# Reordering one turn of a four-layer conditional network: score products and exponentials, the gate's row and logits, and the turned attention output

## The reference, cut to what matters

```
x = x + (einsum('bnh,boh->bno', x, W[subject]) + b[subject])          # 1: a linear map chosen per sequence
x = x + (zX * lap_x(x) + zY * lap_y(x) + zR * x * (1 - x))            # 2: reaction and diffusion
q = (side + b_self) @ Wq + bq                                         # 3: attention, 16 heads of 16
k, v = keys and values of x (masked by seq_len) and of side itself
score = concat([q . k_x (masked), q . k_own]) / 4
weights = softmax(score); attn = weights[..., :-1] @ v_x + weights[..., -1:] * v_own
x = x + (attn @ Wo + bo)
eo, s0, s1 = relu(x @ wi[label]) @ wo[label], relu(x @ swi[e]) @ swo[e]   # 4: one chosen, two shared experts
w = softmax(relu(concat(eo[0], s0[0], s1[0]) @ g1) @ g2)              # gate from token 0 of each
x = x + (eo * w0 + s0 * w1 + s1 * w2)
```

## Time and profile before

| | us |
|---|---|
| median of 3 runs (1175.56 to 1177.09) | 1176.9 |
| the profiled execution | 1179.7 |
| its span in the trace | 1177.9 |
| PE busy in the span | 1028.2 (87%) |
| DVE / ACT / POOL busy | 818.1 / 682.4 / 634.3 |
| one turn of the loop (H0 to the next H0) | 68.24 |

### The profile page before, as it was taken

The page is one execution under the profiler, slowest core; times in us unless marked ns, Lnnn a source line. Parts: engine busy times, 40 slices in busy tenths (PEclk is TensorE's granted clock), DMA queues, the critical chain, the costliest instruction groups (busy, mean ns, idle before and its releaser), DMA issues.

```text
span 1177.9 us, 27595 instructions
## 1 busy us (share of the span) xinstructions
PE 1028.2 (87%) x9488; PEld 955.5 (81%) x9488; DVE 818.1 (69%) x1616; ACT 682.4 (58%) x1401; POOL 634.3 (54%) x544
## 2 busy tenths in 40 slices
PE   3658989999898999899899999989989998998986
PEld 3347878888888888888788888878888887888886
DVE  3475776777777777767777776777777777867632
ACT  2463655747466564746566574656657475665632
POOL 5492645637464564736466473646647364654531
PEclk8667998999999999999999999999999999999978
DMA  4636152171524216152522615242251624234110
GB/s 137 114 108 99 45 67 72 37 124 36 63 77 70 78 47 115 36 69 82 64 72 52 109 36 83 78 54 72 58 104 36 91 70 54 72 63 73 38 45 9
DMA packets 91387, 82.67 MB, mean 70 GB/s; under 512 B 11972, under 2 KB 90852, under 8 KB 91364
## 3 DMA queue, kind: packets, MB, share of 16 engines
q1 hardware_dynamic: 91364, 82.37, 34.8%
HBM read 52.58 MB, written 4.20 MB: 48 GB/s over the span
## 4 chain that ended last, share of the span: by engine, by line
POOL 30%; issue 27%; PE 23%; DVE 13%; ACT 5%; DMA 1%; POOLq 1%; SPq 0%; DVEq 0%; ACTq 0%
POOL exp_lo L1151 10%; POOL prob_lo L1208 10%; PE out L520 3%; DVE prob_lo L1007 3%; PE out L522 3%; PE out L521 3%; PE hid L520 2%; PE hid L521 2%; PE hid L522 2%; PE front L520 2%; POOL e_out L1180 2%; PE front L522 2%; PE front L521 1%; POOL s_lo L1161 1%; PE pv L578 1%
## 5 line engine op out<-in xcount | busy, mean ns | idle before, releaser
L520 PE MATMUL hid<-x_hi,exp_hi 128*128 128x256 f32 x768 | 239.9, 312 | 1.4 <-DVE x_lo L1063 1.4
L1208 POOL TENSOR_TENSOR prob_lo<-prob,prob_hi 128x512 f16<-128x512 f32 x144 | 182.8, 1270 | 88.3 <-ACT prob_hi L837 87.1
L520 PE MATMUL out<-hid_hi,exp_hi 128*128 128x256 f32 x768 | 229.2, 298 | 0.0
L522 PE MATMUL hid<-x_hi,exp_lo 128*128 128x256 f32 x768 | 225.7, 294 | 0.0
L521 PE MATMUL hid<-x_lo,exp_hi 128*128 128x256 f32 x768 | 225.7, 294 | 0.0
L1151 POOL TENSOR_TENSOR exp_lo<-raw,exp_hi 128x512 fp32r<-128x512 f32 x128 | 163.8, 1290 | 109.7 <-ACT exp_hi L849 109.7
L987 DVE TENSOR_REDUCE s_max<-front 128x2 f32<-128x512 f32 x256 | 171.6, 687 | 68.9 <-PE front L623 67.1
L521 PE MATMUL out<-hid_lo,exp_hi 128*128 128x256 f32 x768 | 215.4, 280 | 0.0
L522 PE MATMUL out<-hid_hi,exp_lo 128*128 128x256 f32 x768 | 215.2, 280 | 0.0
L873 ACT ACTIVATE hid_hi<-hid 128x512 fp32r<-128x512 f32 x192 | 115.4, 601 | 168.4 <-PE hid L522 167.0
L1067 DVE SCALAR_TENSOR_TENSOR hid_lo<-hid,hid_hi 128x512 fp32r<-128x512 f32 x192 | 131.5, 685 | 104.0 <-ACT hid_hi L873 102.2
(11 more groups left out here) (162 smaller groups left out, 2311.1 us busy)
## 6 DMA issues: line engine op xcount, KB each, us to landing
raw<-in_wi SPq DMA_DIRECT2D x64, 256.0 KB, 3.7
raw<-in_wo SPq DMA_DIRECT2D x64, 256.0 KB, 2.9
q_rows<-w_raw SPq DMA_DIRECT2D x80, 128.0 KB, 4.3
k_rows<-x1T SPq DMA_DIRECT2D x48, 128.0 KB, 6.6
k_rows<-x_raw SPq DMA_DIRECT2D x48, 128.0 KB, 7.9
x_raw<-in_x SPq DMA_DIRECT2D x16, 256.0 KB, 3.1
w_raw<-in_w SPq DMA_DIRECT2D x16, 256.0 KB, 2.8
s_raw<-in_side SPq DMA_DIRECT2D x16, 256.0 KB, 3.7
```

The source lines that it names most:

```text
L520: nc.tensor.matmul(acc, w_hi, a_hi, start=first, stop=False)
L522: return nc.tensor.matmul(acc, w_lo, a_hi, start=False, stop=last)
L1208: nc.gpsimd.tensor_tensor(prob_lo[:, h % NPROB, :], prob[:, h % NPROB, :], prob_hi[:, h % NPROB, :], ALU.subtract).then_inc(prob_split_poo ...
```

## The change

Only the tables change, and the way the attention output is turned over.

- PE: two hidden products first (`H0 H1 S0 S1 P0` for `H0 S0 S1 H1 .. P0`); the exponential scores are set apart by expert products (`E0 S12 P4 E1` for `E0 S12 E1 P4`, and so on to E6), but E5 E6 and E14 E15 now stand together; `ks` goes from ahead of `pvend` to behind `aT`; the end of the turn is `gate wo logits vp self` for `vp wo gate self logits`.
- ACT, DVE and POOL follow. DVE makes `gate2` ahead of `aT`, then `relu wo logits x3_parts mix scale`, and only then `vp` and `self`. `gate1` goes from ahead of `x2_parts` to behind E11, `gate0` behind H7, `half` ahead of H9. POOL makes E10 ahead of `qa`; ACT makes E12 ahead of `qb` and aT ahead of vs.
- SP: the DMA of `m0` stands ahead of the load of `wo3`.
- `aT` writes chunk c into PSUM bank c (`pv[:, c, 0:256]`) and not both into bank 0, and ACT signals each chunk, so that DVE can begin on chunk 0 while ACT works on chunk 1.

```diff
 PE_BODY = """
-H0 S0 S1 H1 S2 S3 P0 S4 S5 H2 S6 S7 P1 H3 S8 S9 P2 m0 H4 S10 S11 P3 H5
-E0 S12 E1 P4 E2 S13 H6 E3 S14 P5 E4 S15 H7 E5 P6 E6 m1 H8 E7
-x1 P7 q E8 H9 E9 lap P8 E10 H10 E11 E12 kp E13 P9 E14 H11 E15 P10 ks pvend P11
-vs aT vp wo gate self logits
+H0 H1 S0 S1 P0 S2 S3 H2 S4 S5 P1 S6 S7 H3 S8 S9 P2 m0 H4 S10 S11 P3 H5
+E0 S12 P4 E1 S13 H6 E2 S14 P5 E3 S15 H7 E4 P6 E5 E6 H8 m1 E7
+x1 P7 q E8 H9 E9 lap P8 E10 H10 E11 E12 kp E13 P9 E14 E15 H11 P10 pvend P11
+vs aT ks gate wo logits vp self
 """.split()
 ACT_BODY = """
-H0 wi0 x3_keep H1 wi1 H2 wi2 wi3 H3 wo0 m0 H4 wo1 x_parts P3 H5 w_parts E0 E1 wo2 E2 H6 E3 wo3 E4 H7 E5 s_parts E6 m1 H8 E7
-x1_parts react q E8 P7 H9 E9 qa E10 x2_parts H10 E11 qb E12 kp E13 kq E14 H11 E15 ks P11
-vs aT vp x3_parts x2b logits sum
+H0 wi0 H1 x3_keep wi1 H2 wi2 wi3 H3 m0 wo0 H4 wo1 x_parts P3 H5 w_parts E0 wo2 E1 H6 E2 wo3 E3 H7 E4 s_parts E5 E6 m1 H8 E7
+x1_parts react q E8 P7 H9 E9 qa E10 x2_parts H10 E11 E12 qb kp E13 kq E14 E15 H11 P11
+aT vs ks x3_parts logits vp x2b sum
 """.split()
 DVE_BODY = """
-S0 S1 H0 S2 S3 H1 S4 S5 S6 H2 S7 S8 H3 S9 x_parts S10 H4 S11 S12 H5 E1 S13 gate0 H6 S14 E3 S15 H7 E5 H8 E7
-x1 x1_parts react H9 half lap gate1 x2_parts H10 E11 kp E13 k3 H11 E15
-att aT gate2 vp wo x3_parts relu self logits mix scale
+H0 S0 S1 H1 S2 S3 S4 S5 H2 S6 S7 S8 S9 H3 S10 S11 H4 H5 S12 S13 E1 H6 S14 S15 E3 H7 gate0 x_parts E5 H8 E7
+x1 x1_parts react half H9 lap x2_parts H10 E11 gate1 kp E13 k3 E15 H11
+att gate2 aT relu wo logits x3_parts mix scale vp self
 """.split()
 POOL_BODY = """
-wi0 wi1 wi2 wi3 wo0 x_parts wo1 w_parts E0 wo2 E2 wo3 E4 s_parts E6 m1 x1 E8 E9 qa E10 norm qb E12 E14 ks vp sum
+wi0 wi1 wi2 wi3 wo0 x_parts wo1 w_parts E0 wo2 E2 wo3 E4 s_parts E6 m1 x1 E8 E9 E10 qa norm qb E12 E14 ks vp sum
 """.split()
 SP_BODY = """
-load wo0 wo1 wo2 wo3 m0 m1 wi_load E15 kp k3 sum
+load wo0 wo1 wo2 m0 wo3 m1 wi_load E15 kp k3 sum
 """.split()
...
@@ transposed (PE)
-                        last = nc.tensor.transpose(psum[:, c * S + t * P:c * S + (t + 1) * P],
-                                                   src[:, t, c * P:(c + 1) * P], ident[:, :])
+                        last = nc.tensor.transpose(psum[:, c, t * P:(t + 1) * P], src[:, t, c * P:(c + 1) * P], ident[:, :])
...
-                    transposed(pv_bank[0], att).then_inc(att_turned, 1)
+                    transposed(pv, att).then_inc(att_turned, 1)
...
@@ aT (ACT)
-                        last = nc.scalar.activation(ak_hi[:, c, :], psum[:, c, :], ACT.Identity, bias=vec[:, c, BV:BV + 1])
-                    last.then_inc(att_hi_done, 1)
+                        nc.scalar.activation(ak_hi[:, c, :], pv[:, c, 0:S], ACT.Identity, bias=vec[:, c, BV:BV + 1]).then_inc(att_hi_done, 1)
...
@@ aT (DVE)
-                    wait(dve, att_hi_done, 1, j, 1)
...
+                    for c in range(C):
+                        wait(dve, att_hi_done, C, j, c + 1)
+                        last = nc.vector.scalar_tensor_tensor(ak_lo[:, c, :], pv[:, c, 0:S], vec[:, c, BV:BV + 1],
```

More of the change, by code:

```diff
@@ L106 @@
 SHARED = len(SHARED_AT)
-SP_FIRST = "load wo0 wo1 wo2 wo3 m0 E0 E2 E4 E6 m1 wi_load E15 kp k3 vp sum".split()
+SP_FIRST = "load wo0 wo1 wo2 m0 wo3 E0 E2 E4 E6 m1 wi_load E15 kp k3 vp sum".split()
 assert [x for x in SP_FIRST if x in SP_BODY] == SP_BODY
@@ L861, in rest @@
                     wait(act, att_turned, 1, j, 1)
-                    psum = chunked(pv_bank[0])
                     for c in range(C):
-                        last = nc.scalar.activation(ak_hi[:, c, :], psum[:, c, :], ACT.Identity, bias=vec[:, c, BV:BV + 1])
-                    last.then_inc(att_hi_done, 1)
+                        nc.scalar.activation(ak_hi[:, c, :], pv[:, c, 0:S], ACT.Identity, bias=vec[:, c, BV:BV + 1]).then_inc(att_hi_done, 1)
                 elif name[0:2] in ("wi", "wo"):
@@ L1044, in rest @@
                 if name == "aT":
-                    wait(dve, att_hi_done, 1, j, 1)
-                    psum = chunked(pv_bank[0])
                     for c in range(C):
-                        last = nc.vector.scalar_tensor_tensor(ak_lo[:, c, :], psum[:, c, :], vec[:, c, BV:BV + 1],
+                        wait(dve, att_hi_done, C, j, c + 1)
+                        last = nc.vector.scalar_tensor_tensor(ak_lo[:, c, :], pv[:, c, 0:S], vec[:, c, BV:BV + 1],
                                                               ak_hi[:, c, :].bitcast(F32), ALU.add, ALU.subtract)
```

## The result

The changed kernel takes 1139.2 us (median of 4 runs, 1135.6 to 1143.6), where the kernel before took 1176.8 beside it: a ratio of 0.968, interval 0.965 to 0.972. The gain is 37.6 us where 58.5 was forecast.

A forecast was written before the change was run, and what follows sets the result against it. PE's work plus its waits, 5.7 us in six places, were taken to bound the 68.24 us turn; the terms summed to 3.9 us less per turn, 58.5 in all, giving 1118.4 us, range 1095 to 1144.

The forecast's parts named there:

- B: End of the turn: the waits at the logits and the output product go, 2.1 us less per turn.
- D: Stretch of the first eight exponentials: products placed between them cover most of a 1.7 us wait; 0.9 us less per turn.
- C1: First hidden product of the turn: the clock no longer falls, it takes 1.51 us, 1.2 us less per turn.
- C2: First hidden product to first exponential: late DMA and late weights on ACT cost 0.3 us more per turn.
- A: Last eight exponentials: kp's wait goes, but head 12's values wait for POOL's chain; 0 per turn.
- rival 1: First hidden product: the clock falls all the same, weak matmuls counting as a wait; 1135 us; chance 0.13.
- Rival 2: Waits move to POOL's chain, SP's DMA and ACT; 2.0 us less per turn, 1146 us; chance 0.15.
- rival 3: Over the whole turn the waits go almost entirely; 5.6 us less per turn, 1095 us; chance 0.15.

The follow-up runs named there:

- E0: Not a run: the step in the kernel's tables for the exponential scores of head 0.
- E6: Not a run: the step in the kernel's tables for the exponential scores of head 6.
- E5: Not a run: the step in the kernel's tables for the exponential scores of head 5.
- E14: Not a run: the step in the kernel's tables for the exponential scores of head 14.
- E7: Not a run: the step in the kernel's tables for the exponential scores of head 7.

## Why the prediction was right or wrong

The time lies in my range, near its slow end, and in part by luck: B gave 0.7 us per turn more than its term and the turns outside 3 us more, which made up for some of what D lost. The turn's shortening is 2.6 where I had 3.9, by these parts (from marks that both kernels have):

| stretch of the turn | before | after | difference | forecast |
| --- | --- | --- | --- | --- |
| head 12 behind E14, to H0 (B) | 16.11 | 13.29 | 2.8 less | 2.1 less |
| H0 to E0 (C1 and C2) | 18.99 | 18.02 | 1.0 less | 0.9 less |
| E0 to x1 (D) | 14.97 | 16.09 | 1.1 more | 0.9 less |
| x1 to head 12 (A) | 18.16 | 18.23 | 0.1 more | 0 |

- **B, the end of the turn: right, its size too small.** Both waits went. The sum had 2.1 with an upper bound of 2.3, and it is 2.8. The waits are 2.1 of it. I had taken the logits at 0.63 and self at 1.04 from rows with stalls in them; undisturbed they take 0.36 and 0.81. That makes 0.5 of the remaining 0.7.
- **C1, the clock: right; its cause is narrowed, not shown.** It is 1.00 through H0 in each of the 13 turns, and H1 begins 1.52 behind it. The weak matmuls of gate, logits and self are still there, self right ahead of H0: parted by full products they don't bring the fall, and rival 1 is out. But the old end brought back two things at once, the wait for relu and the three weak steps side by side, and with them the fall in every turn of its trace. No run has the one without the other. The Trainium skill ("TensorE: Matmul & The Clock Gate") calls the throttled state the default that activity releases; the reading that I made a rival of, that weak matmuls count as little as a wait, is not borne out for weak matmuls between full products; side by side they weren't tried without a wait.
- **C2: right in sum, not in place.** E0 doesn't wait for the DMA. The 0.4 stands at S0, which waits for the rows of k.
- **D, E0 to E7: this is the step that failed.** I looked at PE and ACT there, and at POOL for head 4. Of DVE I had only that gate0 moves behind H7. I didn't ask what it stood ahead of, though the change put gate0 and x_parts right before E5's low part. gate1's two operations of 2.40 beside POOL were in the earlier trace rows. Priced by them, gate0 and x_parts (1.3 to 1.7 in the kernel before) put E5's low part some 3.8 us behind H7's, and P6 no longer stands between E5 and E6: the values of head 5 had to wait. By gate0's own rows in the kernel before it would have been 3.1, a shorter wait:

```profile
613.12 0.40 DVE L1077 TENSOR_SCALAR gate_terms<-gate,e_out 128x256 f32<-128x256 f32 x1
613.56 1.27 DVE L1082 SCALAR_TENSOR_TENSOR gate_terms<-gate,e_out,gate_terms 128x256 f32<-128x256 f32 x1
```

  Measured, E1 gave the 1.4, and the two waits behind E6 and E7 took 0.3 and 2.0. With the old spacing, and with gate0 and x_parts elsewhere, the wait of 2.0 fell away: shown from both sides. In the second case this stretch takes 14.17, 0.8 less than before, nearly the 0.9 of the sum: the size was right for a DVE that has room, and the queue of DVE is what the step left out.
- **The clock, in D.** I wrote that a wait as long as that for E1 is harmless, since the row showed 1.00. One row of one turn was no ground for that. The trace of the kernel before held the counterexample, in turn 2; the first window is the wait for E1, the second lies behind it:

```profile
196.50:199.20 2.70, 0.97 (x9) 0.59 (x8) 1.29 (x2) 2.09 (x4) 2.44 (x3) 0.99 0.00 0
199.20:202.60 3.40, 3.40 (x24) 3.18 (x24) 0.69 (x1) 1.83 (x4) 2.37 (x2) 0.51 0.00 0
```

  With the old spacing the same wait, in the same place, brought the fall in 2 of 13 turns; the wait at head 5 brings it in 4. This is 6 of the missing us.
- **A, the middle: right as a sum.** kp's wait fell to 0.3, head 12 waits 1.0 for POOL, as forecast. But two claims in it are worth less than I made of them. POOL's chain doesn't bind alone: norm out of its way changed the waiting engine's name to DVE and lost 17 us. And gate1's move, for which I had no net price, is worth 22 us in a kernel without head 5's wait.
- **The rest.** 13 turns at 1.3 less gain each are 17 us short, the falls 6 more. Against that, one of the 13 turns of before, turn 2 with its fall behind E1's wait and a longer one at H0, had taken 71.1, 2.9 over the others, which the change saves too, so 50.7 - 17 - 6 + 2.9 = 30.6, and 31.7 was measured. Turns outside gave 10.4 where I had 3.9 for one full turn and 3.5, 7.4. How that 3 divides wasn't looked into.
- **Rivals.** Rival 2, that waits move, is what happened, with its time (1146) nearer than mine, 1118; but none of the three places that it named (POOL's chain, the DMA behind m0, ACT before E1) held it. The time of rival 1 (1135) is the nearest of all, though its fall at H0 didn't come: the time alone can't tell the rivals apart. The time of rival 3 (1095) is one that the change comes near once gate0 stands elsewhere (1105).

## What to carry to other kernels

When an edit moves a long, deferrable operation on a shared engine, list what stands behind it in that engine's queue at the new place and price the operation at its slowest measured duration; the gain of the move is decided there. Look for a gap of the engine, not for another full stretch: moving gate0 (2.5 to 2.7 us there) from one full stretch to another changed nothing, into a gap it gave 34 us, with x_parts moved as well. And a wait as long as those that brought a fall here (1.65 us and more; up to 1.2 us none did in the 13 turns) should be priced with a chance of a lower clock behind it, from all turns of a trace and not from one.
